# Layer norm split over two engines: ScalarE writes the normed rows, VectorE makes mean, root and their product

## The reference

```python
x = x + 0.5 * ffn0(norm(x))      # p = 0
x = x + attention0(norm(x))      # linear attention, in p = 1 ahead of the experts
x = x + 0.5 * ffn0(norm(x))      # p = 1
x = x + 0.5 * ffn1(norm(x))      # p = 2
x = x + attention1(norm(x))      # causal softmax attention with rope, in p = 3
x = x + 0.5 * ffn1(norm(x))      # p = 3

def norm(x):                      # over the 128 features of a token
    m = mean(x); v = mean((x - m) ** 2)
    return (x - m) / sqrt(v + 1e-5)

def ffn0(h):  # 24 experts, hidden 512; ffn1: 8 experts, hidden 256, and a shared expert
    top 2 of scores h @ gate_w + gate_b, their softmax as weights
    return sum over the two of weight * (gelu(h @ w1[e] + b1[e]) @ w2[e] + b2[e])

def attention0(h):  # 16 heads of 8 features; q and k through two layers
    q, k = softplus(gelu(h @ w1 + b1) @ w2 + b2);  v, g = gelu(h @ w + b)
    out = (q (k^T v) * scale + v) / (q . sum(k) * scale + 128) * g
    return out @ p_w + p_b
```

## Time and profile before

| | us |
|---|---|
| median of three runs | 1048.32 |
| lowest, highest | 1047.94, 1048.72 |
| span of the profiled execution | 1043.2 |
| PE busy | 905.4 (87%) |
| DVE busy | 569.7 (55%) |
| ACT busy | 484.6 (46%) |
| POOL busy | 497.2 (48%) |

### The profile page before, as it was taken

One profiled execution on the slowest core, in us unless ns is written; L12 is line 12 of the kernel. 1 busy time (PEld: TensorE's weight loads), 2 busy tenths in 40 slices (PEclk: granted clock), 3 DMA queues, 4 the chain that ended last, 5 costly groups with the idle time before them and its releaser, 6 DMA issues.

```text
span 1043.2 us, 26677 instructions
## 1 busy us (share of the span) xinstructions
PE 905.4 (87%) x8696; PEld 789.0 (76%) x8696; DVE 569.7 (55%) x2226; ACT 484.6 (46%) x814; POOL 497.2 (48%) x519
## 2 busy tenths in 40 slices
PE   4757999998999799999999998996899999998670
PEld 2327899976889777899888898883688867888570
DVE  7897500066785065785058400588883888872112
ACT  3333544448634257734345444352528455654320
POOL 0551560271027571035372743577744657277655
PEclk9886999999999899999999999898999999999985
DMA  9765999973578783488895899944658456669982
GB/s 306 242 205 156 300 308 242 237 203 95 123 191 231 187 212 104 118 208 234 218 254 146 209 274 226 230 129 130 153 141 189 124 115 165 142 155 247 258 196 75
DMA packets 278655, 200.19 MB, mean 192 GB/s; under 512 B 146112, under 2 KB 233536, under 8 KB 278400
## 3 DMA queue, kind: packets, MB, share of 16 engines
q1 hardware_dynamic: 262144, 164.90, 63.1%
q0 software_dynamic: 16384, 33.59, 11.2%
HBM read 115.56 MB, written 55.57 MB: 164 GB/s over the span
## 4 chain that ended last, share of the span: by engine, by line
PE 58%; DVE 20%; DMA 8%; issue 5%; ACT 4%; POOL 4%; SPq 1%; DVEq 0%; POOLq 0%; ACTq 0%
PE bank L1425 20%; PE bank L1403 5%; PE bank L1405 5%; PE bank L1404 5%; DMA turned<-rows 4%; PE bank L1291 4%; POOL got L2123 3%; PE bank L1244 3%; DMA got<-y_l,slot_index 3%; PE bank L1263 2%; PE bank L1220 2%; PE bank L1253 2%; PE bank L1422 2%; DVE xn L1708 2%; PE bank L1301 2%
## 5 line engine op out<-in xcount | busy, mean ns | idle before, releaser
L1425 PE MATMUL bank<-second,hid 128*128 128x128 f32 x2560 | 369.7, 287 | 0.0
L2123 POOL DMA_INDIRECT got<-y_l,slot_index x256 | 244.7, 956 | 236.4 <-DMA y_l<-y 114.3
L1425 PEld LDWEIGHTS bank<-second,hid 128*128 128x128 f32 x2560 | 324.7, 195 | 4.7 <-issue 3.0
L2103 POOL DMA_INDIRECT rows<-rows_sent,slot_index x192 | 187.8, 978 | 282.2 <-issue 167.7
L1575 ACT ACTIVATE hid<-bank 128x512 f32<-128x512 f32 x320 | 189.7, 597 | 280.4 <-PE bank L1405 266.0
L1403 PE MATMUL bank<-turned,blocks_l 128*128 128x128 f16 x1280 | 239.7, 222 | 41.1 <-DMA turned<-rows 31.2
L1921 DVE SCALAR_TENSOR_TENSOR x_res<-got,share,x_res 128x128 f32<-128x128 f32 x256 | 77.4, 348 | 319.5 <-DMA got<-y_l,slot_index 312.9
L1405 PE MATMUL bank<-turned,blocks_l 128*128 128x128 f16 x1280 | 239.8, 223 | 0.0
L1404 PE MATMUL bank<-turned,blocks_l 128*128 128x128 f16 x1280 | 239.1, 222 | 0.0
L1403 PEld LDWEIGHTS bank<-turned,blocks_l 128*128 x1280 | 127.6, 100 | 55.4 <-issue 52.7
L1404 PEld LDWEIGHTS bank<-turned,blocks_l 128*128 x1280 | 127.1, 99 | 8.9 <-issue 5.9
(11 more groups left out here) (208 smaller groups left out, 1215.6 us busy)
## 6 DMA issues: line engine op xcount, KB each, us to landing
second<-in_w_dram SPq DMA_DIRECT2D x243, 256.0 KB, 5.3
y_l<-y SPq DMA_DIRECT2D x104, 256.0 KB
second<-in_w_dram SPq DMA_DIRECT2D x192, 128.0 KB
got<-y_l,slot_index POOLq DMA_INDIRECT x256
rows<-set SPq DMA_DIRECT2D x1, 3584.0 KB, 14.9
rows<-set SPq DMA_DIRECT2D x7, 512.0 KB, 6.4
rows<-rows_sent,slot_index POOLq DMA_INDIRECT x192
hid<-in_w_dram SPq DMA_DIRECT2D x9, 256.0 KB, 5.2
```

The source lines that it names most:

```text
L1425: m = t.do.matmul(out, hid[:, at], second[:, at], start=False, stop=(c == C - 1))
L2103: d = g.do.indirect_dma_start(rows_dram[s], at, rows[:, 2 * D * i:2 * D * i + 2 * D], None)
L2123: d = g.do.indirect_dma_start(got_mem[slot][:, col:col + D], None, y_dram[layer][s][layer.team(ev.i)], at)
```

## The change

The last step of the norm, one instruction for each tile of 128 tokens x 128 features, goes from VectorE to ScalarE. ScalarE computes scale times x plus bias with a scale and a bias for each partition, so VectorE makes one more small value, offset = -mean x 1/root, in the space of 4 (or 8) more columns. ScalarE waits for that value (`norm_sized`) and for the slot of `xn`, writes four tiles, and raises `norm_done`. In round 0 the second batch of a pair has no stage on VectorE any more.

```diff
-        "norm_a": [[(VE, 4.0, 0.1)]], "norm_g": [[(VE, 4.0 if ev.p else 1.15 if ev.i % 2 else 5.4, 0.1)]],
+        "norm_a": [[(VE, 2.8, 0.1), (SC, 1.1, 0.15)]], "norm_g": [([(VE, 2.8 if ev.p else 4.3, 0.1)] if norm_lead(ev) == ev else []) + [(SC, 1.1, 0.15)]],
...
-           (VE, "r_share"): 2, (VE, "r_top"): 1, (PE, "split_0"): 3, (PE, "la_second"): -3, (PE, "r_rank"): 0.5,
+           (VE, "r_share"): 2, (VE, "r_top"): 1, (PE, "split_0"): 3, (PE, "la_second"): 2, (PE, "r_rank"): -0.5,
...
-        norm_mem = slots("norm", 2, (11 * 2 * BT,))
+        norm_mem = slots("norm", 2, (12 * 2 * BT,))
...
+            def apply_norm(ev):
+                lead = norm_lead(ev)
+                at, xn, x = BT * (ev.i - lead.i), xn_mem[plan.xn.at[ev]], x_res[ev.s]
+                _, rstd, offset, _ = norm_parts(lead)
+                a.wait_ge(*norm_sized[ev.s].after(lead))
...
+                for i in range(BT):
+                    m = a.do.activation(xn[:, D * i:D * i + D], x[:, BT * ev.i + i, :], ACT.Identity,
+                                        bias=offset[:, at + i:at + i + 1], scale=rstd[:, at + i:at + i + 1])
+                m.then_inc(norm_done[ev.s].sem, 1)
...
                 then(v.do.scalar_tensor_tensor(rstd, sq, 1.5 * 3 / 8, rstd, ALU.add, ALU.mult))
-
-            def norm(ev):
...
-                for i in range(BT):
-                    mean, root = mean_var[:, 2 * (at + i):2 * (at + i) + 1], rstd[:, at + i:at + i + 1]
-                    m = v.do.tensor_scalar(xn[:, D * i:D * i + D], x[:, BT * ev.i + i, :], mean, root, ALU.subtract, ALU.mult)
-                m.then_inc(norm_done[ev.s].sem, 1)
+                v.do.scalar_tensor_tensor(offset, mean[:, :, 0], -1.0, rstd, ALU.mult, ALU.mult).then_inc(norm_sized[ev.s].sem, 1)
```

More of the change, by code:

```diff
@@ L967, in xt_of, with norm_parts @@
             return xt_mem[plan.xt.at[Ev("turn_" + role, *ev[1:])]]
+        def norm_parts(lead):
+            n, sm = BT * (norm_end(lead).i + 1 - lead.i), norm_mem[plan.norms.at[lead]]
+            return sm[:, 0:2 * n], sm[:, 2 * n:3 * n], sm[:, 3 * n:4 * n], sm[:, 4 * n:12 * n]
         def halves(rows):
@@ L1061, in macaron_program @@
         w1_part = signal("w1_part", PE, split_0=1, split_1=1)
+        norm_done = signals("norm_done", SC, norm_a=1, norm_g=1)
         xt_done = signals("xt_done", SC, turn_a=1, turn_g=1)
@@ L1487, in copy_turned @@
                 a.do.activation(xt, bank_of(ev)[:, :], ACT.Copy).then_inc(xt_done[ev.s].sem, 1)
+            def apply_norm(ev):
[3 more added lines that the diff above has]
+                a.wait_ge(*norm_sized[ev.s].after(lead))
+                old = plan.xn.before[ev]
+                if old and old.kind == "l2":
+                    a.wait_ge(*expert_out[old.s].after(old))
+                elif old:
+                    turn = Ev("turn_" + old.kind[-1], *old[1:])
+                    a.wait_ge(*turned[old.s].after(turn))
+                    if turn.kind == "turn_g":
+                        a.wait_ge(*rows_high[old.s].after(turn))
+                        a.wait_ge(*rows_low[old.s].after(turn))
+                for i in range(BT):
+                    m = a.do.activation(xn[:, D * i:D * i + D], x[:, BT * ev.i + i, :], ACT.Identity,
+                                        bias=offset[:, at + i:at + i + 1], scale=rstd[:, at + i:at + i + 1])
+                m.then_inc(norm_done[ev.s].sem, 1)
             def high_rows(ev):
@@ L1588, in scalar_program @@
                 kind = ev.kind if ev else None
-                if kind == "turn_a":
+                if kind in ("norm_a", "norm_g"):
+                    apply_norm(ev)
+                elif kind == "turn_a":
                     copy_turned(ev, "a")
@@ L1661, in split_w1, with norm @@
                     m.then_inc(w1_low.sem, 1)
-            def roots(ev, batches, mean_var, rstd, others):
+            def norm(ev):
+                batches = range(ev.i, norm_end(ev).i + 1)
                 n = BT * len(batches)
+                mean_var, rstd, offset, others = norm_parts(ev)
                 stats, var, sq = others[:, 0:6 * n], others[:, 6 * n:7 * n], others[:, 7 * n:8 * n]
+                mean = mean_var.rearrange("p (t v) -> p t v", v=2)
                 old = plan.norms.before[ev]
@@ L1677, in roots @@
                 then(m)
-                then(v.do.tensor_scalar(var, mean_var.rearrange("p (t v) -> p t v", v=2)[:, :, 1], EPS, None, ALU.add))
+                then(v.do.tensor_scalar(var, mean[:, :, 1], EPS, None, ALU.add))
                 then(v.do.tensor_scalar(rstd.bitcast(I32), var.bitcast(I32), -0.5, float(RSQRT_GUESS), ALU.mult, ALU.add))
```

8 lines of the change are left out of this document (5 added, 3 removed).

## The result

The changed kernel has a median of 1057.62 us over seven runs (1050.55 to 1063.03), the kernel before one of 1048.32 over seven (1044.24 to 1051.54). The ratio is 1.0087, 95% interval 1.0056 to 1.0117. The forecast was 1045.7 us, in a range from 1038 to 1055: the sign and the range were both missed. Ratios leave out executions that took over 1.5% more than the fastest of the same kernel beside them.

A forecast was written before the change was run, and what follows sets the result against it. TensorE was taken to bound the kernel wherever its operands are there. Terms A to G summed to -2.6 us, taking the profiled execution from 1043.2 to 1040.6 and the median to 1045.7; the 8-in-10 range was 1038 to 1055.

The forecast's parts named there:

- The price of a norm: Each norm: VectorE relieved by 0.9 us, four ScalarE tiles taking 1.5; where TensorE waits for the norm alone, 0.6 longer.
- E: Into round 3: -4.0 us (-7 to +1), from a relieved VectorE queue, a recovered clock and covered waits.
- F: Rest of the attention, 741 to 945 us: -3.5 us (-8 to +4), from VectorE's relief of 12.8 us.
- B: First stream into round 1: +2.0 us (0 to +6), for a waited-for norm, ScalarE's full block and later ranks.
- C: Second stream into round 1: 0 us (-1.5 to +3), ranks two steps earlier offsetting the norms and ScalarE's block.
- D: Gates of round 2: +1.2 us (0 to +3), two turnings waiting for the norm at 0.6 each.
- rival 1: Slower: ScalarE's in-order queue delays 20 of about 40 norms by 0.6 us, 12 us in all, giving 1055.3 us; chance 0.28.
- rival 2: More gain: VectorE waits from 705 to 945 nearly all close (E and F -12), ranks cost nothing at B, 1039; chance 0.12.
- A: The start: +0.7 us (-3 to +3), the first expert step waiting behind stream 1's ranks.
- that chain as unmoved: At the start, the chain to the first scatter at 63.60 was taken as not moving, though `xt` came some 3 us later.
- that -0.9: Into round 3: with a shorter wait the clock may hold, and half of 1.8 us on four products comes back.
- half of 8.25 + 1.7: Rest of the attention: 5.0 us gained from TensorE's idle time and low clock, 1.5 of it going back at norms.

The follow-up runs named there:

- old_order_2: Kernel before with its order and costs kept, ScalarE writing all norm tiles, repeated where before took 1048 us: 1.0237 of before.
- busy_wait: Kernel before plus four unread tiles on ScalarE at each norm's place in rounds 1 to 3, ScalarE first waiting for the finished norm: 1.0273 of before.
- act_p0: Order of the kernel before, with ScalarE writing the norm's tiles in round 0 only (8 norms): 1.0042 of before.
- ranks_only: Kernel before with the new table of 24 ranks and nothing else, the norm staying on VectorE at its old costs: 1.0139 of before.
- act_p3: Order of the kernel before, with ScalarE writing the norm's tiles in round 3 only (16 of 48 norms): 1.0027 of before.
- before_again: The kernel before, unchanged, profiled a second time on a chip where it takes longer: one execution of 1166.1 us, median 1169.2 us.
- old_order: Kernel before with its planner costs and rank table kept, each norm's tiles written by ScalarE, on a slower chip: 1.0221 of before.

## Why the prediction was wrong

**The price of a norm was right.** 0.67 us later where I had 0.6; 1.65 for the tiles where I had 1.5; VectorE's relief 45.6 where I had 43. (By the page's 1.64 us the sum is 0.79 us later and not 0.75; the trace has 0.67.)

**How often it is bared was wrong, and this is the step that failed first.** I put the 0.6 us on four norms outside E and F (one each in B and C, two in D), those whose longer waits I had read. Every other turning was taken as covered. In the trace of before 19 of the 48 turnings begin within 0.1 us of the last tile of their rows, and 7 more within 0.67 us of it: more than half had less cover than the delay. With ScalarE writing in the order of before (old_order_2) 15 turnings waited for 0.4 us or more instead of 9, and TensorE's time behind `xn` grew by 14 us, before any new rank.

**A term was missing.** What ScalarE's new wait does to the evictions behind it stands in the sum only as 0.5 us in B and as much in C. busy_wait has it without a late norm, at 1.027, and between the products 480 and 560 old_order_2 loses 11.4 us, mostly behind `hid` and to the clock.

Both are rival 1, ScalarE's in-order queue, and its mechanism was right: 12 us on 20 norms was its price, and the split alone costs 2.4%, 25 us. I gave it 0.28. That its 1055.3 us lie near the measured 1057.62 is luck: a loss of twice the size, of which the new order gives back over half. (The sum of rival 2 comes to 1040, not 1039.)

**A (+0.7 forecast, +3.1).** The step that failed is "that chain as unmoved". GpSimd's first scatter came at 36.38 us for 31.34. The one that stood at 63.60 (the seventeenth, not the first, as the prediction has it) came at 67.06. The first expert product started 6.2 us late, and the ranks placed ahead of it waited 6.36 us at 94.59 in place of 1.39 behind it. The slip is ScalarE's tiles and not the new ranks: act_p0 and old_order_2, in the order of before, are 3.4 us late at product 40 as well, and ranks_only is 1.5 us early there. In act_p0 nothing of it is left at product 480, and the run still costs 0.4%. ScalarE's start shows `xt` 2.6 us later than before (15.45 against 12.83), near the 3 us that I had worked out and then set at nothing:

```profile
10.21 1.65 ACT L1512 ACTIVATE xn<-x_res,norm 128x128 f32<-128x128 f32 x4 [8.18 <-DVE norm L1719]
...
15.45 0.57 ACT L1495 ACTIVATE xt<-bank 128x512 f32<-128x512 f32 x1
...
67.06 0.96 POOL L2113 DMA_INDIRECT rows<-rows_sent,slot_index  x1 [10.08 <-DVE slot_index L1851]
```

**B (+2.0, +1.9).** Right in size; the wait ahead of the next first expert is 9.02 us in place of 6.76, as a chain of later ranks would have it.

**C (0, +4.3) and D (+1.2, +6.2).** The ranks two steps earlier were credited with what the norms and ScalarE's block cost, and they did not pay. New waits came for ScalarE (3.44 at 397.54 where it had been 1.92, 2.34 at 448.05 where there had been none) and for `xn` (4.38 at 548.82 in place of 1.40). Of D's 6.2 us 3.0 are that one turning, against 0.6 that I had there; the norm explains 0.67 of it. For the rest, the statistics began 0.62 us before TensorE fell idle, where before they began 2.93 us before it: the gathered rows came later against TensorE's work, and why I have not taken apart.

**E (-4.0, -0.9).** The wait at the first norm of round 3 did shrink, from 4.82 to 2.51 (and 0.60 at 714.07). The clock did not come back: four products took 3.78 us at 727.16 at a granted clock of 0.50 (1.2 GHz), the same as before, so that -0.9 was nothing. The waits in between grew (2.67 at 737.38 where before had 1.65).

**F (-3.5, -0.2).** The step that failed is "half of 8.25 + 1.7". VectorE's share of 79% was read as VectorE being what TensorE waits for there. The relief came in full and TensorE's idle time stayed (8.25 and 8.09 us); act_p3, with the relief and no new rank, is 0.3% slower, not faster.

**The median from the span.** I took the profiled execution to be a typical one, 5.1 us under the median, where 1.3 us is what lies around a span and the rest was a fast run. For a difference of the two that cancels, and it did no harm here, but it says how much one trace can stand off.

**What stays open.** Why the new order loses 1.5 to 2% with VectorE writing. TensorE waits longer for the ranks there; no run took that away, so it is not shown to be the cause. A wait for a slot of `xn` is not. How the loss of the changed kernel divides between late norms and blocked evictions is open too.

## What to carry to other kernels

Where the engines work in order from a fixed plan, a stage that gets longer on the path between two engines can be bare at far more places than the trace shows long waits for: here 26 of 48 turnings had less slack than the 0.67 us that were added. Measure the slack of every instance, and price the change by all that have less of it than the delay. Ask as well what stands in the queue behind the new wait. Relief on an engine with a high busy share can be worth nothing, as it was here, where other waits took its place. An order with tuned ranks is a point of its own: measure the split and the new order as four corners, since each looked like the culprit when only one was undone.

## What the runs showed of the hardware

The same program took 1046 us on some chips and 1169 to 1183 on others. A large part of it is idle time for which the profile shows no releaser ("issue"): in TensorE's groups it was 6.3 us in the first trace of before and 78.4 in the second, VectorE's 4.6 and 118.9. TensorE's busy time was 948.7 against 905.4, too. This idle time stands ahead of products that otherwise follow each other at once; the product of the experts' second layer, in the trace of before_again, has 12.0 us of it where before had none:

```profile
L1425 PE MATMUL bank<-second,hid 128*128 128x128 f32 x2560 | 379.9, 290 | 12.0 <-issue 11.9
```

What caused it I don't know. The changed kernel's ratio was the same on both kinds (1.009 and 1.010), and old_order's too (1.022 and 1.024).

An activation with a scale and a bias per row costs 490 ns for 128x128 in the mean of 168, against 367 with one such operand; four in a row take 1.65 us, where VectorE's four took 1.11.

```profile
L1512 ACT ACTIVATE xn<-x_res,norm 128x128 f32<-128x128 f32 x168 | 69.1, 490 | 50.2 <-DVE norm L1719 50.2
```
